# Output of a grouped-convolution chain: relay and interleaving against two passes of 32x32 transposes

## The chip, the cores and the metric

The kernel runs on one core of a Trainium2 chip. The metric is the device time of one execution in microseconds (us), the median of several.

## The reference, cut to what matters

The input x is 32 batches of 128 channels by 2048 positions, float32. Four layers are applied one after the other, each with a residual:

```
x = x + conv(x, w0, 9 taps, pad 4, groups=4) + (cond @ cw0.T + side)   # L0
x = x + einsum(agg_w1[b], x[b]) + agg_b1[b]                            # L1
x = x + einsum(agg_w2[b], x[b]) + agg_b2[b]                            # L2
x = x + conv(x, w3, 9 taps, pad 4, groups=4) + (cond @ cw3.T + side)   # L3
```

In L1 and L2 agg_w[b] is a 128x128 matrix for each batch: a softmax over 8 attention weights (from a small network on cond) mixes 8 given matrices. Each group of the convolutions maps 32 channels to 32.

## The kernel before

**Work on TensorE.** The residuals are folded into the weights, and L1 and L2 become one matrix per batch, the product (I + A2)(I + A1). A group of 32 channels fills only 32 rows of the 128x128 array. So the positions are split into PH = 4 phases, l = 4s + p with S = 512, and a matmul with 32 rows (one group) and 128 columns gives 32 output channels at all four phases at once. Each array quarter works on one group; four such matmuls run beside each other. A convolution is SHIFTS = 12 shifts by 3 products (operands are split into a high and a low part in the type fp32r: hi*hi, hi*lo, lo*hi), hence 36 rounds of four matmuls of 512 columns. Its result for group g stands in PSUM bank g; partition (p, o) or (o, p) is channel o of the group at phase p, column s. mix has 12 rounds and turns this layout back, so that z has channels on partitions and phase planes along them. The last convolution (conv3, weights of l = 0 or 1: l = 1 here) orders its 128 outputs as (o, p): partition 4o + p.

**The output before.** conv3's four banks are evacuated with their bias to out_taps by ScalarE (g = 0, 1) and VectorE (g = 2, 3; evac_out, lines 401 and 518). Four DMAs on SP's queue (relay_out, line 258) copy each group's 128x512 into 32 rows of out_planes (128 channels, 4 planes of 512). GpSimd copies out_planes to out_sb, interleaving the planes (weave_out, line 333, writes every fourth element), and SP stores out_sb, 1 MB, contiguous (line 267). The last batch has relays with semaphores of their own, and ScalarE and VectorE each weave a half (lines 306 to 319, 409, 669 to 673).

**The input before.** SP loads x[b] to x_in (line 253). GpSimd copies it to x_planes, four phase planes (plane_x, line 325, reads every fourth element). ScalarE rounds it to x_hi (high_x, line 378), VectorE subtracts to get x_lo (low_x, line 493). For x[0] VectorE makes the planes, in halves (line 602).

**Order of the work.** Each engine has its own written-out order, and semaphores tie them. In step t (t = 0 to 32):

- TensorE: conv0(t), first half of conv3(t-1), product(t+1), second half of conv3(t-1), mix(t). conv0(t) waits for x_lo(t) and for the evacuation of t-2; conv3(t-1) for z_lo(t-1); product(t+1) for the mixing matrices of t+1 and for y_lo(t); mix(t) for y_lo(t), the spread weights and the sum of the product.
- ScalarE: high_y(t), high_x(t+2), evac_out(t-1), high_z(t).
- VectorE: mix_matrices(t+1) (16 small instructions, line 526; the one for k = 7, l = 0 writes every fourth element), low_y(t), split_product(t+1) (sum, rounded part, rest), low_x(t+2), evac_out(t-1), low_z(t).
- SP: relay_out(t-2), load_x(t+4), store(t-2), spread_mix_w(t+1).
- GpSimd: plane_x(t+2), weave_out(t-2).

y is the result of conv0, z that of mix. Before the steps stand the set-up of weights and tables and the first batch: tap_blocks (line 557) makes block-diagonal tap matrices, taps_low (line 567) the low part of the turned taps. For l = 0 it writes and reads runs of 32 neighbouring elements, for l = 1 every fourth (phase_columns, line 240).

Of the kernel before, what the change touches and what calls it, by code (L numbers as in the profile page):

```python
# [31 lines left out]
G = 4  # L32
GC = C // G
TAPS, PAD = 9, 4
PH = C // GC
# [6 lines left out]
RELAY = G * DMA  # L42
# [4 lines left out]
def conditioned_residual_kernel(nc, x, cond, side, conv0_w, ctx0_w, mix1, mix2, conv3_w, ctx3_w, out):  # L47

# [4 lines left out]
    with ctx:  # L53
# [7 lines left out]
        x_planes = sb("x_planes", [C, PH, S])  # L61
# [30 lines left out]
        o0, o1 = out_sb[0], out_sb[1]  # L92
# [13 lines left out]
        op = out_planes[:, :, :].rearrange("c p s -> c (p s)")  # L106
# [4 lines left out]
        mix2_in = out_taps[:, 0:G // 2, :].rearrange("o g (k i) -> o (g k) i", i=C)  # L111
# [60 lines left out]
        x0_planed = sem("x0_planed")  # L172
        x0_high = sem("x0_high")
        x_loaded = [sem(f"x_loaded{i}") for i in range(2)]
        x_planed = sem("x_planed")
# [17 lines left out]
        out_relaid = sem("out_relaid")  # L193
        out_woven = sem("out_woven")
        last_relaid = [sem(f"last_relaid{g}") for g in range(G)]
        last_woven = [sem(f"last_woven{h}") for h in range(2)]
# [55 lines left out]
        def _(sp):  # L252
            def load_x(t, d):
                b = t.i + d
                sp.wait_ge(x_planed, b - 1)
                sp.dma_start(x_in[t.par(d)][:, :], x[b]).then_inc(x_loaded[t.par(d)], DMA)

            def relay_out(t, d):
                b = t.i + d
                sp.wait_ge(out_act, 2 * (b + 1))  # L260
                sp.wait_ge(out_dve, 2 * (b + 1))
                wait(sp, out_woven, b)
                for g in range(G):
                    sp.dma_start(out_planes[rows(g), :, :], out_taps[:, g, :])\
                      .then_inc(out_relaid, DMA)
# [16 lines left out]
            def one(t):  # L282
                if t.has(-2) and not t.at(N + 1):
                    relay_out(t, -2)
                if t.has(4):
                    load_x(t, 4)
                if t.has(-2) and not t.at(N + 1):
                    store(t, -2)
                if t.has(1):
                    spread_mix_w(t, 1)  # L290
# [9 lines left out]
            load_x(zero, 2)  # L300
            load_x(zero, 3)
            spread_mix_w(zero, 0)
            for t in ALL:
                one(t)

            b = N - 1
            for g in range(G):
                if g < 2:
                    sp.wait_ge(out_act, 2 * b + g + 1)
                else:  # L310
                    sp.wait_ge(out_dve, 2 * b + g - 1)
                if g == 0:
                    sp.wait_ge(out_woven, b)
                sp.dma_start(out_planes[rows(g), :, :], out_taps[:, g, :])\
                  .then_inc(last_relaid[g], DMA)
            for h in range(2):
                sp.wait_ge(last_woven[h], 1)
                sp.dma_start(out[b, :, h * L // 2:(h + 1) * L // 2], out_sb[b % 2][:, h * L // 2:(h + 1) * L // 2])\
                  .then_inc(out_stored[b % 2], DMA)
            sp.wait_ge(out_stored[0], DMA * (N // 2))  # L320
            sp.wait_ge(out_stored[1], DMA * (N // 2 + 1))

        @block.gpsimd
        def _(pool):
            def plane_x(t, d):
                b = t.i + d
                pool.wait_ge(x_loaded[t.par(d)], DMA * (t.pair(d) + t.par(d)))
                pool.wait_ge(x_lo_done, b)
                pool.wait_ge(x_hi_done, b)
                pool.tensor_copy(x_planes[:, :, :], x_in[t.par(d)][:, :].rearrange("c (s p) -> c p s", p=PH))\  # L330
                    .then_inc(x_planed, 1)

            def weave_out(t, d):
                b = t.i + d
                pool.wait_ge(out_relaid, RELAY * (b + 1))
                wait(pool, out_stored[t.par(d)], DMA * t.pair(d))
                pool.tensor_copy(out_sb[t.par(d)][:, :].rearrange("c (s p) -> c p s", p=PH), out_planes[:, :, :])\  # L337
                    .then_inc(out_woven, 1)

            def one(t):  # L340
                if t.has(2):
                    plane_x(t, 2)
                if t.has(-2) and not t.at(N + 1):
                    weave_out(t, -2)

# [24 lines left out]
            plane_x(Step(0, 0), 1)  # L370
            for t in ALL:
                one(t)
# [4 lines left out]
        def _(act):  # L377
            def high_x(t, d):
                b, p = t.i + d, t.par(d)
                act.wait_ge(x_planed, b + 1)  # L380
                wait(act, conv0_done, G * (b - 1))
                act.activation(x_hi[p][:, :, 1:S + 1], x_planes[:, :, :], ACT.Copy).then_inc(x_hi_done, 1)
# [18 lines left out]
            def evac_out(t, d):  # L401
                b = t.i + d
                wait(act, out_relaid, RELAY * b)
# [5 lines left out]
            def weave_last(h):  # L409
                s = slice(0, S // 2)  # L410
                act.activation(out_sb[1][:, 0:L // 2].rearrange("c (s p) -> c p s", p=PH), out_planes[:, :, s],  # L411
                               ACT.Copy).then_inc(last_woven[h], 1)
# [20 lines left out]
            def one(t):  # L433
                if t.has(0) and not t.at(0):
                    high_y(t)
                if t.has(2):
                    high_x(t, 2)
                if t.has(-1):
                    evac_out(t, -1)
                if t.has(0):  # L440
                    high_z(t)

# [17 lines left out]
            for h in range(2):  # L460
                act.wait_ge((x0_planed, x_planed)[h], 1)
                s = slice(h * S // 2, (h + 1) * S // 2)
                act.activation(x_hi[0][:, :, 1 + s.start:1 + s.stop], x_planes[:, :, s], ACT.Copy)\
                   .then_inc((x0_high, x_hi_done)[h], 1)
# [21 lines left out]
            for g in range(G):  # L486
                act.wait_ge(last_relaid[g], DMA)
            act.wait_ge(out_stored[1], DMA * (N // 2 - 1))
            weave_last(0)

        @block.vector
        def _(dve):
            def low_x(t, d):
                b, p = t.i + d, t.par(d)
                dve.wait_ge(x_hi_done, b + 1)
                dve.tensor_tensor(out=x_lo[p][:, :, 1:S + 1], in0=x_planes[:, :, :],  # L496
# [21 lines left out]
            def evac_out(t, d):  # L518
                b = t.i + d
                wait(dve, out_relaid, RELAY * b)  # L520
                for g in range(2, G):
                    dve.wait_ge(conv3_done, G * b + g + 1)
                    dve.tensor_scalar(out_taps[:, g, :], ps[:, bank(t, d) + g, :],
                                      bias_tab[:, b, G + g:G + g + 1], None, ALU.add).then_inc(out_dve, 1)
# [18 lines left out]
            def split_product(t, d):  # L543
                b = t.i + d
                dve.wait_ge(prod_done, G * (b + 1))
                wait(dve, mix_w_spread[t.par(d - 1)], RELAY * (t.pair(d - 1) + 1) if not (t.at(-d)) else 0)
# [32 lines left out]
            def one(t):  # L579
# [8 lines left out]
                if t.has(-1):  # L588
                    evac_out(t, -1)
# [12 lines left out]
            for h in range(2):  # L602
                dve.wait_ge(x0_halves[h], DMA)
                dve.tensor_copy(x_planes[:, :, h * S // 2:(h + 1) * S // 2],
                                x_in[0][:, h * L // 2:(h + 1) * L // 2].rearrange("c (s p) -> c p s", p=PH))\
                   .then_inc((x0_planed, x_planed)[h], 1)
# [3 lines left out]
            dve.wait_ge(x_planed, 1)  # L610
            for h in range(2):
                dve.wait_ge((x0_high, x_hi_done)[h], 1)
                s = slice(h * S // 2, (h + 1) * S // 2)
                half = dve.tensor_tensor(out=x_lo[0][:, :, 1 + s.start:1 + s.stop], in0=x_planes[:, :, s],
# [36 lines left out]
            dve.wait_ge(x_planed, 2)  # L651
# [17 lines left out]
            for g in range(G):  # L669
                dve.wait_ge(last_relaid[g], DMA)  # L670
            dve.wait_ge(out_stored[1], DMA * (N // 2 - 1))
            dve.tensor_copy(out_sb[1][:, L // 2:L].rearrange("c (s p) -> c p s", p=PH), out_planes[:, :, S // 2:S])\
               .then_inc(last_woven[1], 1)

        @block.tensor
        def _(pe):
# [37 lines left out]
            def mix(t):  # L714
                b, w = t.i, mix_w[t.par(0)]
                pe.wait_ge(y_lo_done, G * (b + 1))
                pe.wait_ge(mix_w_spread[t.par(0)], RELAY * (t.half + 1))
# [159 lines left out]
```

## Time and profile before

| | |
|---|---|
| median of 3 runs | 715.63 us (715.04 to 716.25) |
| profiled execution | 715.86 us |
| its span, first to last instruction | 714.1 us |
| TensorE busy | 664.8 us, 93% |
| VectorE busy | 484.8 us, 68% |
| ScalarE busy | 256.5 us, 36% |
| GpSimd busy | 253.5 us, 36% |
| mean granted TensorE clock | 0.967 |

A busy share is the part of the span in which the engine had at least one instruction running. Matmuls overlap each other, so a busy TensorE is not one at its peak. The chain of waits is followed back from the last instruction: it names at each moment the work that the end depended on. In the table of groups, the time of one instruction is from start to end; instructions on one engine overlap at their ends, so n of them take less than n times that. Line numbers (L683) are those of the kernel above.

### The profile page before, as it was taken

Reading aid. Unit: us, or ns where it says so; the run is one execution under the profiler, and the core shown is the slowest. Engines: PE = TensorE matmul, PEld = TensorE weight load, DVE = VectorE, ACT = ScalarE, POOL = GpSimd, SP = SyncE. Lnnn points to the kernel's source line nnn. Section 1 sums busy time; section 2 is a strip of 40 time slices with the busy share of each in tenths; the row PEclk is TensorE's granted clock in tenths of the full one; section 3 lists DMA queues with packets and bytes.
Section 4 is the critical chain, followed back from the end, with each engine's and each line's share of the span. In section 5 each row is a group of like instructions: output and inputs, shape, how many; then the busy total and the mean of one; then the engine's idle time right before and its main releaser. Section 6 shows DMA issues by size and latency. Waiting matters only on the chain.

```text
span 714.1 us, 24424 instructions
## 1 busy us (share of the span) xinstructions
PE 664.8 (93%) x11104; PEld 650.9 (91%) x11104; DVE 484.8 (68%) x941; ACT 256.5 (36%) x319; POOL 253.5 (36%) x94
## 2 busy tenths in 40 slices
PE   4846999999999999999999999999999999999970
PEld 4645889999999999999999999999999999999960
DVE  5378677767676667776777776787777777777221
ACT  3303433343334443434333444343443344432211
POOL 7022233343344444334334444433433444422220
PEclk9957999999999999999999999999999999999986
DMA  8131478889988888889998888888999888666666
GB/s 274 61 90 31 114 184 194 182 155 206 175 181 187 192 192 190 189 166 176 206 174 182 187 192 191 190 185 163 180 206 180 171 192 194 134 131 128 109 120 152
DMA packets 50238, 119.72 MB, mean 168 GB/s; under 512 B 5865, under 2 KB 25369, under 8 KB 42265
## 3 DMA queue, kind: packets, MB, share of 16 engines
q1 hardware_dynamic: 48592, 118.66, 77.7%
q10 hardware_dynamic: 1352, 0.57, 0.3%
q8 instruction: 22, 0.36, 0.3%
q14 instruction: 16, 0.12, 0.1%
q0 software_dynamic: 256, 0.01, 0.0%
HBM read 35.33 MB, written 33.55 MB: 96 GB/s over the span
## 4 chain that ended last, share of the span: by engine, by line
PE 91%; DVE 3%; DMA 2%; ACT 1%; issue 1%; ACTq 0%; SPq 0%; DVEq 0%
PE ps L683 77%; PE ps L724 12%; DMA out_planes<-in_L_cond_c_weight 1%; DMA out_planes<-out_taps 1%; DVE out_planes L561 1%; DVE acc L540 1%; PE ps L711 1%; PE ps L753 1%; DVE y_lo L503 0%; DVE z_lo L513 0%; DVE mat2T L540 0%; ACT out_sb L411 0%; PE ps L778 0%; DVE mat L540 0%; DVE taps_lo L569 0%
## 5 line engine op out<-in xcount | busy, mean ns | idle before, releaser
L337 POOL COPY out_sb<-out_planes 128x2048 f32<-128x2048 f32 x31 | 122.1, 3939 | 301.2 <-DMA out_planes<-out_taps 301.2
L683 PE MATMUL ps<-z_hi,taps_hi 32*128 32x512 f32 x1536 | 203.8, 402 | 3.6 <-DVE z_lo L513 3.6
L683 PE MATMUL ps<-x_hi,taps_hi 32*128 32x512 f32 x1536 | 202.2, 397 | 1.0 <-DVE prod L553 1.0
L683 PE MATMUL ps<-z_hi,taps_lo 32*128 32x512 f32 x1536 | 201.2, 394 | 0.5 <-issue 0.5
L683 PE MATMUL ps<-x_lo,taps_hi 32*128 32x512 f32 x1536 | 200.9, 394 | 0.0
L683 PE MATMUL ps<-x_hi,taps_lo 32*128 32x512 f32 x1536 | 200.7, 393 | 0.0
L683 PE MATMUL ps<-z_lo,taps_hi 32*128 32x512 f32 x1536 | 200.3, 393 | 0.0
L330 POOL COPY x_planes<-x_in 128x2048 f32<-128x2048 f32 x31 | 120.3, 3881 | 138.9 <-DVE x_lo L496 135.8
L388 ACT ACTIVATE y_hi<-ps,bias_tab 128x512 fp32r<-128x512 f32 x128 | 77.6, 690 | 213.5 <-PE ps L683 213.5
L513 DVE SCALAR_TENSOR_TENSOR z_lo<-ps,bias_tab,z_hi 128x1024 fp32r<-128x1024 f32 x64 | 79.2, 1280 | 74.9 <-ACT z_hi L398 74.9
L683 PEld LDWEIGHTS ps<-z_hi,taps_hi 32*128 32x128 f32 x1536 | 120.8, 186 | 6.1 <-DVE z_lo L513 4.0
L683 PEld LDWEIGHTS ps<-x_hi,taps_hi 32*128 32x128 f32 x1536 | 121.2, 186 | 3.0 <-DVE prod L553 1.2
L683 PEld LDWEIGHTS ps<-x_lo,taps_hi 32*128 32x128 f32 x1536 | 121.4, 187 | 1.7 <-issue 0.2
L683 PEld LDWEIGHTS ps<-x_hi,taps_lo 32*128 32x128 f32 x1536 | 121.3, 186 | 1.7
L683 PEld LDWEIGHTS ps<-z_lo,taps_hi 32*128 32x128 f32 x1536 | 121.1, 186 | 1.1
L683 PEld LDWEIGHTS ps<-z_hi,taps_lo 32*128 32x128 f32 x1536 | 120.6, 185 | 1.3
L503 DVE SCALAR_TENSOR_TENSOR y_lo<-ps,bias_tab,y_hi 128x512 fp32r<-128x512 f32 x128 | 87.3, 745 | 46.8 <-ACT y_hi L388 46.8
L724 PE MATMUL ps<-y_hi,mix_w 32*128 32x512 f32 x1024 | 98.9, 394 | 0.0
L406 ACT ACTIVATE out_taps<-ps,bias_tab 128x512 f32<-128x512 f32 x64 | 40.6, 685 | 155.7 <-PE ps L683 155.7
L398 ACT ACTIVATE z_hi<-ps,bias_tab 128x1024 fp32r<-128x1024 f32 x64 | 67.9, 1113 | 46.7 <-PE ps L724 46.7
L724 PEld LDWEIGHTS ps<-y_hi,mix_w 32*128 32x128 f32 x1024 | 72.8, 186 | 0.8
L496 DVE TENSOR_TENSOR x_lo<-x_planes,x_hi 128x2048 fp32r<-128x2048 f32 x31 | 70.8, 2285 | 0.0
(102 smaller groups left out, 566.2 us busy)
## 6 DMA issues: line engine op xcount, KB each, us to landing
out_planes<-out_taps SPq DMA_DIRECT2D x128, 256.0 KB, 7.4
x_in<-in_x SPq DMA_DIRECT2D x31, 1024.0 KB, 11.0
out<-out_sb SPq DMA_DIRECT2D x31, 1024.0 KB, 4.2
mix_w<-prod SPq DMA_DIRECT2D x128, 128.0 KB, 4.5
x_in<-in_x SPq DMA_DIRECT2D x2, 512.0 KB, 6.1
out<-out_sb SPq DMA_DIRECT2D x2, 512.0 KB, 3.1
out_taps<-in_L_cond_weight SPq DMA_DIRECT2D x1, 512.0 KB, 9.5
mix_w<-in_L_cond_weight SPq DMA_DIRECT2D x1, 512.0 KB, 13.2
```

Of the source, the lines that this page charges most:

```text
L330: pool.tensor_copy(x_planes[:, :, :], x_in[t.par(d)][:, :].rearrange("c (s p) -> c p s", p=PH))\
L337: pool.tensor_copy(out_sb[t.par(d)][:, :].rearrange("c (s p) -> c p s", p=PH), out_planes[:, :, :])\
L388: act.activation(y_hi[:, g, :], ps[:, bank(t, 0) + g, :], ACT.Identity, bias=bias_tab[:, b, g:g + 1]).then_inc(y_hi_done, 1)
L398: act.activation(z_hi[:, 2 * h:2 * h + 2, 1:S + 1], ps[:, k:k + 2, :], ACT.Identity, bias=bias_tab[:, b, 2 * G:BIAS]).then_inc(z_hi_done, 1)
L406: act.activation(out_taps[:, g, :], ps[:, bank(t, d) + g, :], ACT.Identity, bias=bias_tab[:, b, G + g:G + g + 1]).then_inc(out_act, 1)
L496: dve.tensor_tensor(out=x_lo[p][:, :, 1:S + 1], in0=x_planes[:, :, :], in1=x_hi[p][:, :, 1:S + 1].bitcast(F32), op=ALU.subtract).then_inc( ...
L503: dve.scalar_tensor_tensor(out=y_lo[:, g, :], in0=ps[:, bank(t, 0) + g, :], scalar=bias_tab[:, b, g:g + 1], in1=y_hi[:, g, :].bitcast(F32) ...
L513: dve.scalar_tensor_tensor(out=z_lo[:, 2 * h:2 * h + 2, 1:S + 1], in0=ps[:, k:k + 2, :], scalar=bias_tab[:, b, 2 * G:BIAS], in1=z_hi[:, 2 ...
L540: dve.scalar_tensor_tensor(out=o, in0=inputs[0], scalar=att_tab[:, b, K * l + k:K * l + k + 1], in1=inputs[1], op0=ALU.mult, op1=ALU.add). ...
L561: dve.tensor_copy(blocks[rows(g), :, rows(g)], conv_in[l][rows(g), :, :].rearrange("o c t -> o t c"))\
L683: tile = pe.matmul(ps[:, first_bank + g, :], w[rows(g), d, :], a[rows(g), d % PH, d // PH:d // PH + S], start=(n == 0), stop=(n == TURNS - 1))
L724: tile = pe.matmul(ps[:, bank(t, 0) + p, :], w[rows(p), g, h, :], a[rows(p), g, :], start=(n == 0), stop=(n == 3 * G - 1))
```

## The change

The output no longer goes through relay and weave. ScalarE evacuates groups 0 and 1 with bias to out_taps as before (now two groups large). VectorE then makes eight 128x512 transposes in 32x32 blocks in step t, in place of its two evacuations. The first pass takes groups 2 and 3 from PSUM, without bias, and 0 and 1 from out_taps, and writes out_turned. The second pass reads out_turned and writes out_runs, in which partition (o, i) holds for each group g the 512 contiguous positions 512i to 512i + 511 of channel o. ScalarE adds the bias of groups 2 and 3 in place (bias_runs). SP stores with one DMA a batch, in runs of 512 elements.

GpSimd has no work in the steps. x_planes is gone: high_x and low_x read x_in at every fourth element. SP's load_x waits for x_lo (b - 1 batches) in place of x_planed. The last batch is stored like the others.

```diff
-        x_planes = sb("x_planes", [C, PH, S])
-        out_taps = sb("out_taps", [C, G, S])
-        out_planes = sb("out_planes", [C, PH, S])
-        out_sb = [sb(f"out_sb{i}", [C, L]) for i in range(2)]
+        out_taps = sb("out_taps", [C, G // 2, S])
+        out_turned = sb("out_turned", [C, G, S])
+        out_runs = [sb(f"out_runs{i}", [C, G, RUN]) for i in range(2)]
...
+        def planes(buf, s):
+            return buf[:, PH * s.start:PH * s.stop].rearrange("c (s p) -> c p s", p=PH)
```

On SP's queue:

```diff
             def load_x(t, d):
                 b = t.i + d
-                sp.wait_ge(x_planed, b - 1)
+                wait(sp, x_lo_done, b - 1)
                 sp.dma_start(x_in[t.par(d)][:, :], x[b]).then_inc(x_loaded[t.par(d)], DMA)
-            def relay_out(t, d):
...
             def store(t, d):
                 b = t.i + d
-                sp.wait_ge(out_woven, b + 1)
-                sp.dma_start(out[b], out_sb[t.par(d)][:, :]).then_inc(out_stored[t.par(d)], DMA)
+                sp.wait_ge(runs_done, G * (b + 1))
+                sp.wait_ge(runs_biased, 2 * (b + 1))
+                sp.dma_start(out[b].rearrange("(g o) (i x) -> (o i) g x", g=G, i=RUNS), out_runs[t.par(d)][:, :, :])\
+                  .then_inc(out_stored[t.par(d)], DMA)
...
             def one(t):
+                if t.has(1):
+                    spread_mix_w(t, 1)
                 if t.has(4):
                     load_x(t, 4)
-                if t.has(-2) and not t.at(N + 1):
-                    store(t, -2)
-                if t.has(1):
-                    spread_mix_w(t, 1)
+                if t.has(-1):
+                    store(t, -1)
```

On ScalarE, where bias_runs(t, -1) is the last call of one(t), after high_z(t):

```diff
-                act.activation(x_hi[p][:, :, 1:S + 1], x_planes[:, :, :], ACT.Copy).then_inc(x_hi_done, 1)
+                act.activation(x_hi[p][:, :, 1:S + 1], planes(x_in[p], slice(0, S)), ACT.Copy).then_inc(x_hi_done, 1)
...
+            def bias_runs(t, d):
+                b = t.i + d
+                for g in range(2, G):
+                    act.wait_ge(runs_done, G * b + g + 1)
+                    o = out_runs[t.par(d)][:, g, :]
+                    act.activation(o, o, ACT.Identity, bias=bias_tab[:, b, G + g:G + g + 1]).then_inc(runs_biased, 1)
```

On VectorE, where turn_out(t, -1) stands in one(t) in the place of evac_out:

```diff
-                dve.tensor_tensor(out=x_lo[p][:, :, 1:S + 1], in0=x_planes[:, :, :],
+                dve.tensor_tensor(out=x_lo[p][:, :, 1:S + 1], in0=planes(x_in[p], slice(0, S)),
...
-            def evac_out(t, d):
...
+            def turned(g):
+                return out_turned[:, g, :].rearrange("c (p o b) -> c b o p", p=PH, o=SQ // PH)
+
+            def turn_out(t, d):
+                b = t.i + d
+                for g in (2, 3, 0, 1):
+                    if g >= 2:
+                        dve.wait_ge(conv3_done, G * b + g + 1)
+                        dve.transpose(turned(g), ps[:, bank(t, d) + g, :]).then_inc(out_dve, 1)
+                    else:
+                        dve.wait_ge(out_act, 2 * b + g + 1)
+                        dve.transpose(turned(g), out_taps[:, g, :]).then_inc(taps_turned, 1)
+                wait(dve, out_stored[t.par(d)], DMA * t.pair(d))
+                for n, g in enumerate((0, 1, 2, 3)):
+                    dve.wait_ge(taps_turned if g < 2 else out_dve, 2 * b + g % 2 + 1)
+                    dve.transpose(out_runs[t.par(d)][:, g, :].rearrange("c (j s p) -> c j p s", s=SQ, p=PH),
+                                  out_turned[:, g, :].rearrange("c (p r j) -> c j p r", p=PH, r=SQ))\
+                       .then_inc(runs_done, 1)
```

SQ is 32, RUNS is 4, RUN is 512. Where the head made x_planes of x[0] in halves, ScalarE and VectorE now read the halves of x_in[0] directly, and load_x of x[3] stands behind the first spread_mix_w on SP's queue.

## Rows read from the trace of the kernel before

**Rows 1.** The chain that ended last, by engine, share of the span.

```profile
PE 91%; DVE 3%; DMA 2%; ACT 1%; issue 1%; ACTq 0%; SPq 0%; DVEq 0%
```

**Rows 2.** The chain in one steady step: start us, us, what.

```profile
401.66 2.79 PE ps L724 x48
404.45 12.54 PE ps L683 x216
416.98 0.14 PE ps L711 x5
417.12 4.31 PE ps L683 x70
```

**Rows 3.** Timeline of VectorE: start us, us, what, [idle before <-releaser].

```profile
405.53 2.48 DVE L513 SCALAR_TENSOR_TENSOR z_lo<-ps,bias_tab,z_hi 128x1024 fp32r<-128x1024 f32 x2 [2.42 <-ACT z_hi L398]
407.92 0.34 DVE L540 SCALAR_TENSOR_TENSOR acc<-mix_w,att_tab,ident 128x128 f32<-128x128 f32 x1
...
411.60 0.43 DVE L540 SCALAR_TENSOR_TENSOR mat<-mix_w,att_tab,acc 128x128 f32<-128x128 f32 x1
...
413.43 2.73 DVE L503 SCALAR_TENSOR_TENSOR y_lo<-ps,bias_tab,y_hi 128x512 fp32r<-128x512 f32 x4 [1.22 <-ACT y_hi L388]
417.27 0.69 DVE L548 TENSOR_REDUCE prod_sum<-ps 128x128 f32<-128x512 f32 x1 [1.12 <-PE ps L711]
...
418.69 2.29 DVE L496 TENSOR_TENSOR x_lo<-x_planes,x_hi 128x2048 fp32r<-128x2048 f32 x1
421.47 1.41 DVE L523 TENSOR_SCALAR out_taps<-ps,bias_tab 128x512 f32<-128x512 f32 x2 [0.49 <-PE ps L683]
...
441.29 0.75 DVE L523 TENSOR_SCALAR out_taps<-ps,bias_tab 128x512 f32<-128x512 f32 x1 [0.58 <-PE ps L683]
```

**Rows 4.** Timeline of ScalarE in a steady step.

```profile
434.79 1.93 ACT L382 ACTIVATE x_hi<-x_planes 128x2048 fp32r<-128x2048 f32 x1
```

**Rows 5.** Windows of taps_lo (L569), l = 0, then l = 1: busy (instructions), clock, DMA.

```profile
11.11:12.66 1.55, 1.55 (x4) 1.00 1.01 372
55.99:58.42 2.43, 2.43 (x4) 0.95 0.00 0
```

**Rows 6.** Line 569 in the window 55 to 58.4 (l = 1), then in the whole trace.

```profile
L569 DVE TENSOR_TENSOR taps_lo<-ps,taps_hi x4: 651/669/690, 56.0 to 57.8; 128x288 fp32r<-128x288 f32 x4
...
L569 DVE TENSOR_TENSOR taps_lo<-ps,taps_hi x8: 447/554/690, 11.1 to 57.8; 128x288 fp32r<-128x288 f32 x8
```

**Rows 7.** Groups of instructions, two with strided operands: busy us, mean ns | idle before.

```profile
L604 DVE COPY x_planes<-x_in 128x1024 f32<-128x1024 f32 x2 | 2.2, 1113 | 2.0 <-DMA x_in<-in_x 2.0
...
L411 ACT ACTIVATE out_sb<-out_planes 128x1024 f32<-128x1024 f32 x1 | 2.0, 2034 | 9.8 <-DMA out_planes<-out_taps 9.8
```

**Rows 8.** The chain: mix(31), then conv3(31).

```profile
678.58 2.73 PE ps L724 x47
...
684.98 11.53 PE ps L683 x126
```

**Rows 9.** DMA issues: KB each, median us from issue to landing.

```profile
out<-out_sb SPq DMA_DIRECT2D x31, 1024.0 KB, 4.2
```

**Rows 10.** The chain in the head.

```profile
17.34 6.57 PE ps L683 x64
...
44.40 3.87 DVE out_planes L561
...
48.30 0.43 DVE out_planes L561
```

**Rows 11.** Timeline of GpSimd in the head.

```profile
44.15 3.84 POOL L330 COPY x_planes<-x_in 128x2048 f32<-128x2048 f32 x1 [25.25 <-DVE x_lo L496]
```

**Rows 12.** Timeline of VectorE in the head.

```profile
12.58 2.35 DVE L614 TENSOR_TENSOR x_lo<-x_planes,x_hi 128x1024 fp32r<-128x1024 f32 x2
```

**Rows 13.** Windows: PE, PEld, DVE, ACT, POOL busy (x), PEclk, DMA share, GB/s.

```profile
34.00:36.00 2.00, 0.00 (x0) 0.00 (x0) 1.92 (x6) 2.00 (x4) 0.00 (x0) 0.93 0.00 0
...
685.00:691.10 6.10, 6.10 (x56) 4.80 (x60) 0.00 (x0) 0.00 (x0) 0.55 (x1) 0.50 0.66 77
```

More of the change, by code:

```diff
@@ L41 @@
 DMA = 16
-RELAY = G * DMA
+SPREAD = PH * DMA
+SQ = 32
+RUNS = 4
+RUN = L // RUNS
 ATT = 2 * K
@@ L89, in conditioned_residual_kernel @@
         ones = sb("ones", [GC, C])
-        o0, o1 = out_sb[0], out_sb[1]
+        o0, o1 = (o[:, :, :].rearrange("c g x -> c (g x)") for o in out_runs)
         conv_in = [o0[:, 288 * l:288 * l + GC * TAPS].rearrange("o (c k) -> o c k", k=TAPS) for l in range(2)]
@@ L192, in conditioned_residual_kernel @@
         out_dve = sem("out_dve")
[L193 to L196, printed above, removed]
+        taps_turned = sem("taps_turned")
+        runs_done = sem("runs_done")
+        runs_biased = sem("runs_biased")
         out_stored = [sem(f"out_stored{i}") for i in range(2)]
@@ L300, in _ @@
             load_x(zero, 2)
+            spread_mix_w(zero, 0)
             load_x(zero, 3)
-            spread_mix_w(zero, 0)
             for t in ALL:
                 one(t)
[L306 to L319, printed above, removed]
             sp.wait_ge(out_stored[0], DMA * (N // 2))
-            sp.wait_ge(out_stored[1], DMA * (N // 2 + 1))
+            sp.wait_ge(out_stored[1], DMA * (N // 2))
         @block.gpsimd
         def _(pool):
[L325 to L344, printed above, removed]
             pool.memset(ident[:, :], 0.0).then_inc(ident_step, 1)
@@ L369, in _ @@
                 pool.dma_start(bias_k[l], m[7]).then_inc(bias_k_in, DMA)
-            plane_x(Step(0, 0), 1)
-            for t in ALL:
-                one(t)
         HALOS = 6
@@ L402, in evac_out @@
                 b = t.i + d
-                wait(act, out_relaid, RELAY * b)
+                wait(act, taps_turned, 2 * b)
                 for g in range(2):
@@ L441, in one @@
                     high_z(t)
+                if t.has(-1):
+                    bias_runs(t, -1)
             act.dma_start(cond_in, cond).then_inc(cond_arrived, DMA)
@@ L460, in _ @@
             for h in range(2):
-                act.wait_ge((x0_planed, x_planed)[h], 1)
+                act.wait_ge(x0_halves[h], DMA)
                 s = slice(h * S // 2, (h + 1) * S // 2)
-                act.activation(x_hi[0][:, :, 1 + s.start:1 + s.stop], x_planes[:, :, s], ACT.Copy)\
+                act.activation(x_hi[0][:, :, 1 + s.start:1 + s.stop], planes(x_in[0], s), ACT.Copy)\
                    .then_inc((x0_high, x_hi_done)[h], 1)
@@ L485, in _ @@
                 one(t)
[L486 to L489, printed above, removed]
         @block.vector
@@ L516, in low_z @@
                                              op0=ALU.add, op1=ALU.subtract).then_inc(z_lo_done, 1)
-            def evac_out(t, d):
+            def turned(g):
+                return out_turned[:, g, :].rearrange("c (p o b) -> c b o p", p=PH, o=SQ // PH)
+            def turn_out(t, d):
                 b = t.i + d
[L520 to L524, printed above, removed]
+                for g in (2, 3, 0, 1):
[11 more added lines that the diff above has]
+                       .then_inc(runs_done, 1)
             def mix_matrices(t, d):
@@ L545, in split_product @@
                 dve.wait_ge(prod_done, G * (b + 1))
-                wait(dve, mix_w_spread[t.par(d - 1)], RELAY * (t.pair(d - 1) + 1) if not (t.at(-d)) else 0)
+                wait(dve, mix_w_spread[t.par(d - 1)], SPREAD * (t.pair(d - 1) + 1) if not (t.at(-d)) else 0)
                 at = prod_at(t, d)
@@ L588, in one @@
                 if t.has(-1):
-                    evac_out(t, -1)
+                    turn_out(t, -1)
                 if t.has(0):
@@ L601, in _ @@
             dve.tensor_copy(condT, ps[:, 6, 0:N]).then_inc(condT_done, 1)
[L602 to L606, printed above, removed]
             for p in range(PH):
@@ L613, in _ @@
                 s = slice(h * S // 2, (h + 1) * S // 2)
-                half = dve.tensor_tensor(out=x_lo[0][:, :, 1 + s.start:1 + s.stop], in0=x_planes[:, :, s],
+                half = dve.tensor_tensor(out=x_lo[0][:, :, 1 + s.start:1 + s.stop], in0=planes(x_in[0], s),
                                          in1=x_hi[0][:, :, 1 + s.start:1 + s.stop].bitcast(F32), op=ALU.subtract)
@@ L650, in _ @@
             split_product(zero, 0)
-            dve.wait_ge(x_planed, 2)
             low_x(zero, 1)
@@ L668, in _ @@
                 one(t)
[L669 to L673, printed above, removed]
         @block.tensor
@@ L716, in mix @@
                 pe.wait_ge(y_lo_done, G * (b + 1))
-                pe.wait_ge(mix_w_spread[t.par(0)], RELAY * (t.half + 1))
+                pe.wait_ge(mix_w_spread[t.par(0)], SPREAD * (t.half + 1))
                 if t.has(1) and not t.at(0):
```

22 lines of the change are left out of this document (3 added, 19 removed).

## The prediction

> **What bounds the kernel now.** I read the page's busy shares and its chain first, then the chain of one step, then VectorE's timeline of the same step, then the two ends of the trace. The chain is TensorE for 91% of the span [rows 1]. In a steady step (401.66 to 421.43, 19.77 us) the chain holds only TensorE: mix 2.79, conv0 and the first half of conv3 12.54, product 0.14, second half of conv3 4.31, with no gap [rows 2]. So a gain can only come from the head and the tail, and a loss from any engine that no longer fits in 19.77 us.
>
> VectorE is that engine [rows 3]. Call E the end of a conv3 (421.43). After it come: evac_out (2 instructions, 1.41), a wait of 2.42 for z_hi, low_z (2.39 until the next start), the 16 instructions of mix_matrices (407.92 to 412.21, which is 413.43 less the 1.22 of waiting: 4.29), low_y 2.73, a wait for the product, split_product (417.27 to 418.69: 1.42), low_x 2.29, and 0.49 of waiting for E. The waits sum to some 5.3 us, but only what lies between E and low_y helps the change, since product(t+1) on TensorE waits for all of low_y(t): low_y ends at 416.16, the product starts at 416.98. Once low_y slips by more than about 0.8 us, TensorE stands still in the middle of conv3, every step.
>
> **The change, part by part.**
>
> *Added: eight 128x512 transposes a step on VectorE*, between E and low_z, in place of two evacuations. No row shows a transpose. Bound from below: of an evacuation of the same size one alone takes 0.75 us and two 1.41, so they repeat every 0.66 us [rows 3]. Bound from above: the nearest strided rows. taps_lo writes 288 elements per partition, for l=0 in rows of 32 neighbours, for l=1 at every fourth element (16 bytes), reading taps_hi in the same way. Four instructions take 1.55 us in the first case and 2.43 us in the second [rows 5]; less the last one's own 0.45 and 0.65 us (the shortest of the eight, and the shortest of the strided four [rows 6]) and over three that is 0.37 and 0.59 us each, so the strided one costs 0.59/288 = 2.05 ns an element. ScalarE shows it too: 1024 elements written at stride 4 took 2.03 us [rows 7], 2048 contiguous ones 1.93 us [rows 4]. The first pass writes with strides of 128, 16 and 1 elements, innermost 128, so no two writes in a row are neighbours; the second reads at stride 16 and writes at stride 4. Both have what the slow row has, hence 512 x 2.05 ns = 1.05, with a little between instructions 1.07 us each, 8.6 us for eight. I take this end, as the rows with the same strides are nearer than the evacuation. That taps_lo has a strided read and write at once and still costs 2.05 ns says that the two do not add up.
>
> The Trainium skill ("SBUF — State Buffer", the note on SBUF cachelines) says that SBUF works in 16-byte lines and wants two hits a line for full rate, so that fp32 at a stride of 16 bytes pays. The strided rows agree. Against it stands the rule of "VectorE: DVE Perf Modes" (Mode 1x) that the basic mode takes any stride at one result a cycle, and of "Vector Engine (DVE) Microarchitecture Reference" (3.8) that the transpose sustains one element per cycle. By those the first rival below would come true; taps_lo is the row against them.
>
> *Moved: x read in its natural order.* POOL's plane_x goes. high_x and low_x now read x_in at stride 4. For low_x the lower bound is today's 2.29, the upper 2048 x 2.05 ns = 4.2, with its start 4.3. The row for a strided read alone is x_planes at the start: 1024 in 1.11 us [rows 7], no slower than one operand in plain order would be at 0.66 us for 512 from PSUM, so it would speak for 2.29; but it is a copy of one operand from SBUF to SBUF, which may otherwise run faster, and so decides nothing. taps_lo, with two operands and strided ones, is the same kind of instruction as low_x. I take 4.3. high_x on ScalarE becomes 1.9 to 3.9; it starts 13.4 us after E (434.79 against 421.43 [rows 4]) and is hidden by VectorE, which comes later still.
>
> *The sum of a step.* From the end of low_y: product starts 0.1 later, reduce 0.29 after that, split_product 1.42, low_x 4.3 (together 6.1, against 0.1 + 0.14 + 4.31 + 0.1 = 4.65 at which conv3's end lets the turn start), turn_out 8.6, low_z 2.39, mix_matrices 4.29, low_y 2.73: 6.1 + 8.6 + 9.41 = 24.1 us. VectorE has no pause in it and sets the step: 24.1 - 19.77 = 4.33 us more. Steps t=1 to 28 have all parts: 28 x 4.33 = +121. Step 29 has no low_x: 4.65 + 8.6 + 9.41 = 22.66, +2.9. Step 30 has neither product nor matrices and stays at TensorE's pace. conv3(31) started 6.4 us after conv3(30) ended (684.98 against 678.58 [rows 8]); now turn_out(30) stands before low_z(31): 0.1 + 8.6 + 2.4 = 11.1, +4.7.
>
> *Removed at the tail: relay and weave.* From the end of conv3(31) (684.98 + 11.53 = 696.51) to the end of the span are 17.6 us: evacuation, four relays, the weave, two half stores [rows 8]. After: 0.1 + 8.6, the last bias_runs 0.7 (as an evacuation on ScalarE), issue and store 0.1 + 0.35 + 4.2 (median landing of a full store [rows 9]) = 14.1. -3.5.
>
> *Head.* tap_blocks(1) stood 3.87 us in one copy that otherwise takes 0.43, [rows 10], all of it under POOL's plane_x at 44.15 [rows 11]: with that gone, -3.4. low_x(1) before it in VectorE's queue grows by 2.0. The two low halves of x(0), 12.58 to 14.93 [rows 12], end 3.1 later (first high half +1.0, their own 2.1), at 18.0; conv0(0) started at 17.34 [rows 10]: +0.7. Net -0.7. Other moves I price at nothing: SP's load_x now waits for x_lo (VectorE, about a step and a half before the data is used, 11 us landing at most); the load of x(3) goes behind spread(0), 30 us ahead of its use; the store goes behind spread and load in SP's queue, and only two steps later does anyone wait for out_runs. bias_runs sits last in ScalarE's step behind turn_out, and behind it high_y, which then waits for conv0 or low_y anyway; if turn_out took over 11 us, high_y would come late. The relays' 1 MB a step leaves the queues, which were hidden.
>
> Sum: 121 + 2.9 + 4.7 - 3.5 - 0.7 = +124.4; 714.1 + 124.4 = 838.5 us of span, and 1.8 us around it (profiled execution 715.86, median 715.63, the same within 0.03%): **840 us**.
>
> **The rivals.**
>
> *All strides free (faster).* Eight transposes at 0.66 = 5.3, low_x 2.3. Then the turn starts at E and the loop is 4.65 + 5.3 + 9.41 = 19.36 < 19.77: TensorE keeps its pace. Gains: head -3.4, tail 17.6 - (0.1 + 5.3 + 0.7 + 4.65) = -6.8, loss before conv3(31) 0.1 + 5.3 + 2.4 - 6.4 = +1.4. 714.1 - 8.8 + 1.8 = 707. For it: the 1.11 us of the strided copy, and mix_matrices' one instruction that writes at stride 4, which at 0.43 in place of 0.34 is only a little slower [rows 3]. Against it: taps_lo. It turns into a loss when a transpose costs over 0.71 us (8T = 19.77 - 4.65 - 9.41), or low_x over 3.25.
>
> *Only one of the two directions is slow.* Only low_x: 6.1 + 5.3 + 9.41 = 20.8, +29 over 28 steps, less the ends: 739. Reads only (first pass 0.66, second 1.07, low_x 4.3): 22.4 a step, 789. Writes only (low_x 2.3): 22.66 a step and the whole gain of the head, 798.
>
> *The clock falls too.* At 24.1 us a step TensorE stands 1.2 us before conv3 and 2.8 us before the product. In the trace it ran at half its rate (1.2 GHz) for 6.1 us after the pause of 3.6 us before conv3(31), about 3 us of work lost; and where TensorE did nothing from before 34.0, the mean of 34 to 36 is already 0.93 [rows 13]. Here that would fall on conv3's second half: its end comes at 7.7 after low_y in place of 4.65, later than low_x's 6.1, so +1.6 a step, 28 x 1.6 = 45: 885 us if it happens in every step, in between if in some.
>
> *Strides of 64 and 512 bytes cost more than 16.* At 1.5 us a transpose the step is 27.5 and the time about 940. No row has such a stride in SBUF.
>
> **Chances.** Forecast (840) 0.42; clock falls as well (up to 885) 0.17; one direction only (789 to 798) 0.15; low_x only (739) 0.05; all strides free (707) 0.14; no net change, gains at the ends against a small excess of the step, 0.02; beyond 895 0.05. The range 735 to 895 leaves out the last three. The forecast's own range is 825 to 860, T from 1.03 to 1.15. Changes within 0.2% cannot be told from none here. Faster 0.14, same 0.02, slower 0.84.
>
> **What would show it.** Right: transposes of about 1.1 us, low_x about 4.3 us, VectorE over 95% busy, TensorE's waits named low_y and low_z, a period near 24 us, tap_blocks(1) in four copies of 0.43. Wrong: transposes of 0.66 us and an unchanged chain of 19.77 us a step (then about 707), or the granted clock at 0.5 for a part of each step. If the transposes take 1.07 and low_x 2.3 the mechanism holds and the time is near 798.

## Result: 799.85 us in place of 715.34

| | before | after |
|---|---|---|
| median, same chip | 715.34 us (714.86 to 716.25) | 799.85 us (797.16 to 805.11) |
| ratio, 95% | | 1.119 (1.113 to 1.125) |
| span of the profiled execution | 714.1 us | 798.6 us |
| mean granted TensorE clock | 0.967 | 0.948 |
| data moved by DMA | 119.7 MB | 86.2 MB |

The change makes the kernel 12% slower. The forecast was 840 us, its range 735 to 895. The direction and the mechanism came true; the size was 40 us too large.

The page after: first the busy shares (us, share of the span, instructions), then the chain by engine, which stands against [rows 1].

```profile
PE 695.2 (87%) x11104; PEld 625.4 (78%) x11104; DVE 711.0 (89%) x1130; ACT 364.0 (46%) x382; POOL 9.4 (1%) x32
...
DVE 75%; PE 18%; issue 4%; ACT 2%; DMA 0%; DVEq 0%; ACTq 0%
```

The chain was TensorE for 91% and is now VectorE for 75%. VectorE's busy time rose from 484.8 to 711.0 us. The page's groups (busy us, mean ns | idle before) say with what: eight transposes a step, of about 1.1 us each, and low_x at 3.8.

```profile
L491 DVE STREAM_TRANSPOSE out_runs<-out_turned 128x512 f32<-128x512 f32 x128 | 128.6, 1107 | 0.0
...
L453 DVE TENSOR_TENSOR x_lo<-x_in,x_hi 128x2048 fp32r<-128x2048 f32 x31 | 119.2, 3845 | 0.3 <-ACT x_hi L339 0.3
...
L484 DVE STREAM_TRANSPOSE out_turned<-ps 128x512 f32<-128x512 f32 x64 | 64.8, 1099 | 27.1 <-PE ps L640 27.1
```

One steady step in the chain (start, us), to be laid beside [rows 2]:

```profile
416.43 2.65 DVE y_lo L460 x4
...
419.12 0.62 PE ps L668 x8
...
419.77 0.70 DVE prod_sum L517
...
421.05 3.75 DVE x_lo L453
424.80 1.94 DVE out_turned L484 x2
426.74 0.97 DVE out_turned L487 x2
427.71 0.65 issue
428.36 4.08 DVE out_runs L491 x4
432.44 2.33 DVE z_lo L470 x2
...
438.97 2.65 DVE y_lo L460 x4
```

From one low_y to the next (416.43 to 438.97) are 22.54 us. Apart from the product of 0.62 us all of it is VectorE (in the "issue" of 0.65 the fourth transpose, which starts at 427.4 and takes 1.12, is running). Where the rows are cut, between 420.47 and 421.05, stand the cast and the rest of the product (0.24 and 0.29), and between 432.44 and 438.97 stand low_z and the 16 instructions of mix_matrices, 6.53 us. The starts of the product's sum are 22.49 to 22.59 us apart in 17 of 29 steps, 22.91 and 22.67 in two, and 23.25 to 23.31 in ten, about every third; before, 19.77 and 19.82 in turn. The mean over t = 1 to 28 is 22.79 against 19.80: 28 x 2.99 = 84 us. That is all of the difference. What the ends give and take cancels out.

TensorE's longest waits (us in total, times, longest):

```profile
PE ps L668 <- DVE y_lo L460: 52.3, 29, 2.0
...
PE ps L640 <- DVE out_turned L484: 5.6, 19, 0.7
```

It stands before the product in every step. Windows behind one such stop, with the columns of [rows 13], show what every third step has besides:

```profile
438.60:442.00 3.40, 1.57 (x35) 1.15 (x30) 3.00 (x6) 3.21 (x1) 0.00 (x0) 1.00 0.00 0
442.00:445.40 3.40, 3.40 (x44) 2.90 (x40) 3.02 (x4) 0.00 (x0) 0.00 (x0) 0.53 0.11 39
445.40:448.80 3.40, 3.40 (x64) 3.07 (x60) 2.78 (x2) 0.82 (x2) 0.00 (x0) 0.97 0.83 135
```

In the first row TensorE works for 1.57 us, stands, and is still granted 1.00. In the second it is busy throughout at a granted 0.53, nearly all of it at 1.2 GHz, and 44 matmuls fall in it where the third, nearly all at 2.4 GHz, has 64.

The two ends. The tail, from the end of conv3(31) at 785.64 to 798.6, takes 13.0 us, 17.6 before [rows 8]:

```profile
774.26 11.38 PE ps L640 x140
785.64 1.90 DVE out_turned L484 x2
...
791.10 1.94 DVE out_runs L491 x2
...
793.07 0.72 ACT out_runs L371
```

The head has lost its stall: the copies of tap_blocks(1) take 0.32 to 0.44 us, where one took 3.87 [rows 10]; low_x(1) before them grew to 3.79.

```profile
41.96 3.79 DVE x_lo L453
45.75 0.32 DVE out_turned L530
...
47.02 0.44 DVE out_turned L530
```

### The profile page after: what moved, and what is told of

The parts are those of the page before. It is cut to its first block, busy times and chain, and to the rows that moved or that the text cites. A ratio compares the mean times of both kernels' runs of the same rounds, so it can differ in the third digit from the quotient of the medians.

```text
span 798.6 us, 24419 instructions
## 1 busy us (share of the span) xinstructions
PE 695.2 (87%) x11104; PEld 625.4 (78%) x11104; DVE 711.0 (89%) x1130; ACT 364.0 (46%) x382; POOL 9.4 (1%) x32
## 4 chain that ended last, share of the span: by engine, by line
DVE 75%; PE 18%; issue 4%; ACT 2%; DMA 0%; DVEq 0%; ACTq 0%
DVE out_runs L491 15%; PE ps L640 14%; DVE y_lo L460 10%; DVE x_lo L453 9%; DVE z_lo L470 9%; DVE acc L509 8%; DVE out_turned L484 8%; DVE mat2T L509 4%; DVE out_turned L487 4%; DVE mat L509 3%; PE ps L668 2%; DVE prod_sum L517 2%; PE ps L710 1%; DVE prod L522 1%; DVE prod L520 1%
## 5 line engine op out<-in xcount | busy, mean ns | idle before, releaser
L640 PE MATMUL ps<-x_lo,taps_hi 32*128 32x512 f32 x1536 | 167.9, 394 | 0.0
L640 PE MATMUL ps<-x_hi,taps_lo 32*128 32x512 f32 x1536 | 167.5, 392 | 0.0
L491 DVE STREAM_TRANSPOSE out_runs<-out_turned 128x512 f32<-128x512 f32 x128 | 128.6, 1107 | 0.0
L339 ACT ACTIVATE x_hi<-x_in 128x2048 fp32r<-128x2048 f32 x31 | 121.4, 3917 | 0.0
L453 DVE TENSOR_TENSOR x_lo<-x_in,x_hi 128x2048 fp32r<-128x2048 f32 x31 | 119.2, 3845 | 0.3 <-ACT x_hi L339 0.3
L640 PEld LDWEIGHTS ps<-x_hi,taps_hi 32*128 32x128 f32 x1536 | 87.9, 186 | 20.1 <-issue 13.7
L640 PEld LDWEIGHTS ps<-x_hi,taps_lo 32*128 32x128 f32 x1536 | 88.2, 186 | 5.5
L640 PEld LDWEIGHTS ps<-x_lo,taps_hi 32*128 32x128 f32 x1536 | 88.1, 186 | 5.0 <-issue 0.2
L484 DVE STREAM_TRANSPOSE out_turned<-ps 128x512 f32<-128x512 f32 x64 | 64.8, 1099 | 27.1 <-PE ps L640 27.1
L355 ACT ACTIVATE z_hi<-ps,bias_tab 128x1024 fp32r<-128x1024 f32 x64 | 68.0, 1115 | 45.8 <-PE ps L681 45.8
L371 ACT ACTIVATE out_runs<-out_runs,bias_tab 128x512 f32<-128x512 f32 x64 | 46.4, 725 | 87.6 <-DVE out_runs L491 87.6
```

What stands on the lines that cost most here:

```text
L339: act.activation(x_hi[p][:, :, 1:S + 1], planes(x_in[p], slice(0, S)), ACT.Copy).then_inc(x_hi_done, 1)
L355: act.activation(z_hi[:, 2 * h:2 * h + 2, 1:S + 1], ps[:, k:k + 2, :], ACT.Identity, bias=bias_tab[:, b, 2 * G:BIAS]).then_inc(z_hi_done, 1)
L371: act.activation(o, o, ACT.Identity, bias=bias_tab[:, b, G + g:G + g + 1]).then_inc(runs_biased, 1)
L453: dve.tensor_tensor(out=x_lo[p][:, :, 1:S + 1], in0=planes(x_in[p], slice(0, S)), in1=x_hi[p][:, :, 1:S + 1].bitcast(F32), op=ALU.subtract ...
L484: dve.transpose(turned(g), ps[:, bank(t, d) + g, :]).then_inc(out_dve, 1)
L491: dve.transpose(out_runs[t.par(d)][:, g, :].rearrange("c (j s p) -> c j p s", s=SQ, p=PH), out_turned[:, g, :].rearrange("c (p r j) -> c j ...
```

## Experiments

Each ran beside the kernel before on its chip; the ratio is to that, with a 95% interval.

**1. All eight transposes plain.** Is it the number of transposes or their strides?

```diff
-dve.transpose(turned(g), ps[:, bank(t, d) + g, :])
+dve.transpose(out_turned[:, g, :], ps[:, bank(t, d) + g, :])
...
-dve.transpose(out_runs[..][:, g, :].rearrange("c (j s p) -> c j p s", s=SQ, p=PH),
-              out_turned[:, g, :].rearrange("c (p r j) -> c j p r", p=PH, r=SQ))
+dve.transpose(out_runs[..][:, g, :], out_turned[:, g, :])
```

> The changed kernel with all eight transposes reading and writing plain runs of 512 (the output's order is then not the reference's). Theory (the stride is the price, not the transpose): a transpose repeats every 0.66 us in place of 0.95, the clean step goes from 22.5 to 22.5 - 8 x 0.29 = 20.2 us, the span to about 720 (28 steps at 20.2 in place of 22.8 on average: -73, step 29, low_z(31) and the tail -2.3 each). Rival A (a transpose costs 0.95 us whatever its operands): 800 us unchanged. Rival B (half of the price is the transpose's own): near 760.

Measured: 716.34 us, ratio 1.002 (1.000 to 1.003). The steps take 20.12 us. VectorE's timeline of one turn:

```profile
404.31 1.32 DVE L484 STREAM_TRANSPOSE out_turned<-ps 128x512 f32<-128x512 f32 x2
405.54 1.27 DVE L487 STREAM_TRANSPOSE out_turned<-out_taps 128x512 f32<-128x512 f32 x2
406.73 2.46 DVE L491 STREAM_TRANSPOSE out_runs<-out_turned 128x512 f32<-128x512 f32 x4
```

Eight follow each other in 4.8 us (404.31 to 409.10), 0.60 each, in place of 7.64 and 0.95. Taking the strides away, with the same number of instructions on the same data, gives back all but 1 us of 84. So the cost is the transposes' strides. low_x, strided and 3.86 us long here too, costs these steps at most the 0.3 us by which they exceed 19.80, and the shorter ends make up for it; beside strided transposes, where VectorE has no time to spare, it costs more (experiment 3).

**2. One stride for each transpose.** Which strides, and do reading and writing add up?

```diff
+if g == 3: return out_turned[:, g, :].rearrange("c (p o b) -> c b o p", p=PH, o=SQ // PH)
+if g == 2: return out_turned[:, g, :]
+return out_turned[:, g, :].rearrange("c (x h) -> c h x", h=(4, 2)[g])
...
+if g >= 2: o = o.rearrange("c (j s p) -> c j p s", s=SQ, p=PH)
+if g % 2:  i = i.rearrange("c (p r j) -> c j p r", p=PH, r=SQ)
```

> Eight transposes with different strides in one kernel, to read each by itself (the output's order is not the reference's). First pass writes: group 2 plain, 3 strides 16 and 128, 0 every fourth element (16 bytes), 1 every second (8 bytes); reads plain. Second pass: 0 plain to plain, 1 reads strided and writes plain, 2 reads plain and writes strided, 3 both strided. Theory (each access that leaves its 16-byte line is slow, reading or writing, and the two don't add): 0.66 us for plain and for every second element, 0.95 for all others. Rival A (only writes are slow): group 1 of the second pass 0.66. Rival B (any stride is slow): the write at every second element 0.95. Rival C (they add): group 3 of the second pass above group 2.

Measured: 757.79 us in a single run. The instructions of one step by themselves (ns least/median/most):

```profile
L488 DVE STREAM_TRANSPOSE out_turned<-ps x1: 701/701/701, 405.7 to 405.7; 128x512 f32<-128x512 f32 x1
```
```profile
L491 DVE STREAM_TRANSPOSE out_turned<-out_taps x1: 683/683/683, 408.2 to 408.2; 128x512 f32<-128x512 f32 x1
```
```profile
L500 DVE STREAM_TRANSPOSE out_runs<-out_turned x1: 1076/1076/1076, 409.4 to 409.4; 128x512 f32<-128x512 f32 x1
```
```profile
L500 DVE STREAM_TRANSPOSE out_runs<-out_turned x1: 1115/1115/1115, 411.2 to 411.2; 128x512 f32<-128x512 f32 x1
```

In this order: plain on both sides (from PSUM); write at every second element; strided read with a plain write; both strided. The others are a write at every fourth element (1080), one at strides of 16 and 128 elements (1095), plain on both sides in the second pass (666) and a plain read with a write at every fourth (1070). So 8 bytes from one element to the next cost nothing (in writing), 16 bytes cost 0.4 us per 512 elements, a write with steps of 64 and 512 bytes no more than one at 16, reading at 16 bytes as much as writing, and both together no more than one. The rivals "larger strides cost more" (for writes) and "one direction only" fall here. A first pass with plain writes and a second that reads with steps of 128 and 4 elements gave no time, so whether a read with such large steps costs more stays open.

**3. The output change alone, GpSimd still making x_planes.** It takes low_x back to 2.28 us and puts a long GpSimd copy beside the transposes.

```diff
+pool.tensor_copy(x_planes[:, :, :], x_in[b % 2][:, :].rearrange("c (s p) -> c p s", p=PH))
...
-in0=planes(x_in[p], slice(0, S)),
+in0=x_planes[:, :, :],
```

> The changed output, but from x[1] on GpSimd makes x_planes as before, so high_x and low_x read plain planes. Theory (strided read of x is a term of its own): low_x 2.3 us in place of 3.85; the turn then starts at conv3's end, so only 0.8 of the 1.5 us is won: clean step 21.7 us, and GpSimd's copy stands again in front of tap_blocks(1) for 3.4 us: about 773 us. Rival (GpSimd's copies hold up VectorE's strided instructions as well): low_x 2.3 us but transposes over 0.95 us in the windows of the copies, 785 us or more.

Measured: 783.67 us, ratio 1.095 (1.093 to 1.097). The transposes beside the copy are hardly longer (2.10, 2.04 and 3.99 us for the three groups in one step, against medians of 2.03, 2.00 and 4.02 in the changed kernel), so the rival's cause is not there. Undisturbed steps take 21.8 us, as expected, against 22.5 with low_x strided; but 8 of 29 take 23.2 to 23.4, each with a fall of the clock. The mean is 22.2, and the 11 us above the expectation lie in these steps.

**4. The input change alone.** The kernel before, only x read directly; the load of x moves to the end of each step's DMA issues on SP's queue.

```diff
-            def plane_x(t, d):
...
-in0=x_planes[:, :, :],
+in0=planes(x_in[p], slice(0, S)),
```

> The kernel before with one half of the change alone: x split from its natural order (no x_planes, no plane_x), relay and weave as before. From the changed kernel's trace low_x repeats after 3.8 us and high_x takes 3.9. Theory (VectorE has room for this part): low_x ends 1 us after conv3's end, evac_out right after it ends when mix ends, low_z is not delayed: step 19.8 as before, head -3.4 (tap_blocks(1)) + 1.5 (low_x(1)): 713 us. Rival (the late evacuation holds back conv0, which needs its PSUM banks): up to 0.3 us a step, 722 us. The prediction's rival had 739 for this part, from a low_x of 4.3 us and eight transposes at 0.66 us beside it.

Measured: 776.18 us, ratio 1.085 (1.083 to 1.086). The theory's 713 and the rival's 722 were both over 50 us too low, the prediction's 739 for this part 37. The timeline of one step names what none of them had:

```profile
429.46 3.91 POOL L329 COPY out_sb<-out_planes 128x2048 f32<-128x2048 f32 x1 [18.00 <-DMA out_planes<-out_taps]
...
431.08 2.37 DVE L540 CAST prod<-prod_sum 128x128 fp32r<-128x128 f32 x1
```

The cast of the product's sum, 128 elements, takes 2.37 us and ends at 433.45, 0.08 us after GpSimd's weave copy (433.37). Over the whole trace, then over that of the changed kernel, where GpSimd copies nothing in the steps:

```profile
L540 DVE CAST prod<-prod_sum x32: 226/1274/2734, 42.1 to 717.7; 128x128 fp32r<-128x128 f32 x32
```
```profile
L520 DVE CAST prod<-prod_sum x32: 226/228/229, 41.5 to 739.7; 128x128 fp32r<-128x128 f32 x32
```

In this run 28 of the 32 casts overlap a weave copy, and each of them ends 0.07 to 0.09 us after it. The cast waits for the copy to end. The Trainium skill ("SBUF — State Buffer", Who interferes with whom) has this rule: casts and copies of VectorE may want the port pair that it shares with GpSimd, and whoever holds it has it for the whole instruction. The trace agrees, up to 2.73 us in place of 0.23. The kernel before shows it too, with casts of up to 1.42 us that end 0.07 to 0.09 us after a weave copy, but its chain does not run through them. In this kernel the late cast delays low_x (now 3.84), that delays the evacuation, and conv0 waits for its banks (the first of TensorE's waits):

```profile
PE ps L665 <- DVE out_taps L512: 34.9, 27, 2.1
```

Behind that stop the clock falls in every second step (0.57 from 440 to 444): steps of 20.4 to 20.9 and of 23.4 to 23.8, mostly in turn.

**5. The same, with the weave held back until low_x is done.** If it is the cast, this takes nearly all away. SP issues the store behind the spread and the load, which is not part of the question.

```diff
 pool.wait_ge(out_relaid, RELAY * (b + 1))
+if t.has(2):
+    pool.wait_ge(x_lo_done, t.i + 3)
```

> e5 (the kernel before with x read directly), with GpSimd's weave_out(t-2) held until low_x(t+2) is done, so that it no longer runs beside split_product's cast or low_x; on SP's queue the store goes behind spread_mix_w and load_x. Theory (e5's steps of 20.7 and 23.6 us come from VectorE's cast, which waits 1 to 2 us for GpSimd's copy, with the clock's fall behind it, and not from reading x at stride 4): the cast back at 0.23 us, all steps 19.8 to 19.9, 713 to 716 us. Rival A (the slower low_x alone makes evac_out late and conv0 waits for its banks): cast 0.23 us, but steps of 20.1 or more, over 722 us. Rival B (the lock moves to the mixing matrices): their first instruction 2 us instead of 0.34, time near 770.

Measured: 723.67 us, ratio 1.013 (1.009 to 1.016).

```profile
L542 DVE CAST prod<-prod_sum x32: 226/227/229, 40.9 to 663.6; 128x128 fp32r<-128x128 f32 x32
```

Some 53 of the 61 us were the waiting cast and the falls of the clock behind it. What is left, steps of 20.21 us on average, has another chain:

```profile
416.42 1.84 ACT y_hi L379 x3
418.25 3.78 ACT x_hi L373
...
422.06 2.49 DVE x_lo L487
...
425.81 1.43 DVE out_taps L514 x2
...
427.38 12.65 PE ps L667 x205
```

high_x, 3.9 us long, keeps low_x waiting, that the evacuation, and that conv0. Both theories held a part.

**6. The product three rounds later in conv3** (after round 21 in place of 18). The changed kernel, nothing else; VectorE's work is the same.

```diff
-            MID = TURNS // 2
+            MID = TURNS // 2 + 3
```

> The changed kernel with product(t+1) three rounds later in conv3 (MID 21 in place of 18): the same work, TensorE's pause before the product 0.7 us shorter (1.9 to 1.2), the rest of it moved before conv0. VectorE's instructions are unchanged. Theory (the steps of 23.3 us among those of 22.5 come from the clock, which falls after pauses of 1.9 us): no falls, every step 22.5, 800 - 8 = 791 to 792 us. Rival (the 0.75 us have another cause, such as a queue): 800 us as before.

Measured: 788.56 us, ratio 1.103 (1.101 to 1.105), 11 us less than the changed kernel. The steps take 22.43 to 22.54 us. TensorE's single stop has become two (in brackets, us):

```profile
399.69 0.51 PE L640 MATMUL ps<-x_hi,taps_hi 32*128 32x512 f32 x4 [0.96 <-DVE out_turned L484]
```
```profile
PE ps L668 <- DVE y_lo L460: 33.5, 29, 1.3
PE ps L640 <- DVE out_turned L484: 27.1, 29, 1.0
```

The sum of the stops is the same or larger (60.6 against 57.9 us), but no step has a fall of the clock (mean granted clock 0.972 against 0.948). So the long steps of the changed kernel come from the stop being in one piece of up to 2.0 us, and cost it some 10 us. The runs fit its length as the cause: in experiment 2 the stop is in one piece too, but of 1.0 to 1.2 us, and no clock falls there either.

**7. First pass plain, ScalarE evacuates all four groups.** Half of the strides gone, with the right output, by storing in 16 DMAs.

```diff
-def turned(g): return out_turned[:, g, :].rearrange("c (p o b) -> c b o p", p=PH, o=SQ // PH)
+dve.transpose(out_turned[:, g, :].rearrange("c (j k x) -> c k j x", j=4, k=4), out_taps[:, g, :])
...
-sp.dma_start(out[b].rearrange("(g o) (i x) -> (o i) g x", g=G, i=RUNS), out_runs[..][:, :, :])
+for n in range(16):
+    sp.dma_start(out[b].rearrange("(m o) (k x) -> m k o x", m=16, k=RUNS)[n], out_runs[..][rows(n % 4), n // 4, :])
```

> The changed kernel with a first pass that writes plain runs of 32 elements; the second reads and writes every fourth. For that the partitions of out_runs come in another order, so the store is 16 DMAs a batch, and ScalarE evacuates all four groups with their bias (no bias_runs). Same output as the reference. Theory (strides do not add within an instruction, a pass made plain is a clear gain): first pass 0.62 us each, second 0.95, clean step 22.5 - 1.3 = 21.2 us with no fall of the clock, about 753 us. Rival (16 stores on SP's queue hold up spread_mix_w and mix): step above 22, 775 us or more.

Measured: 762.14 us, ratio 1.065 (1.063 to 1.067).

```profile
403.41 2.49 DVE L472 STREAM_TRANSPOSE out_turned<-out_taps 128x512 f32<-128x512 f32 x4
405.81 4.06 DVE L477 STREAM_TRANSPOSE out_runs<-out_turned 128x512 f32<-128x512 f32 x4
```

The first pass costs 0.60 each, the second 0.97, and the step 21.27 us, as expected: the price per stride sets the time here too. The miss of 9 us is nearly all in the tail: from the end of conv3(31) at 740.57 to 760.6 are 20.0 us, since SP issues 16 stores one after the other, in 10.5 us (747.64 to 758.13).

**8. Only the ends of the change, in the kernel before.** Steps as before with relay and weave; the last batch alone goes through the eight transposes and four stores, and GpSimd's copy of x[2] waits until tap_blocks(1) is done.

```diff
+if b == 2:
+    pool.wait_ge(blocks_step, 2 * (2 + G) - 1)
...
-                if t.has(-1):
+                if t.at(N):
+                    turn_last(t)
+                elif t.has(-1):
                     evac_out(t, -1)
```

> The kernel before, its steps untouched, changed only at the ends: the last batch is put in order by the eight transposes, with a store for each group as soon as it is done, in place of relay and weave, and plane_x(2) waits until tap_blocks(1) is through. Theory (the change's gain is real but lies at the ends): head -3.4, tail from 17.6 to 7.6 + 0.4 + 3 = 11, -6.6: 705 us. Rival A (the tail is bound by the landing of the stores): 708 to 710. Rival B (the head's stall has another cause than GpSimd's copy): 3.4 more than the theory.

Measured: 706.22 us against 715.35, ratio 0.985 (0.983 to 0.987), the fastest of all. The chain of its tail:

```profile
695.71 1.25 DVE out_planes L525 x2
...
701.21 1.93 DVE out_sb L532 x2
```

The last batch goes out in four stores, one for each group, landing 2.1 us after issue (median); the tail from 695.66 to 705.8 takes 10.1 us in place of 17.6. The steps stay at 19.8. In the head the second tap_blocks has copies of 0.42 to 0.44 us. The first lost something in this execution: one copy took 4.11 us, beside GpSimd's clearing of the tap buffers, where all four took 2.09 before. So conv0(1) starts only 1.15 us earlier (63.08 in place of 64.23). Whether the 4.11 are due to the edit wasn't tried; the times of this kernel spread from 703.4 to 707.6 us.

## Why the prediction was right, and where it missed 40 us

**VectorE becomes the bound, through low_y and the product: right.** The chain, the wait named y_lo in all 29 steps, and the first experiment show it. The pause before conv3 that it also forecast (1.2 us) is absent in the steps. TensorE waits a little for PSUM banks before conv0 instead (out_turned, 5.6 us in all): conv0(t+1) needs the banks that the first pass empties, a wait that the prediction did not list. Its sign "VectorE over 95% busy" holds in the steady steps, where VectorE stands 0.70 of 22.5 us, and not over the whole span (89%).

**The price of a stride: the mechanism right, the size too high.** A transpose counted 1.07 and repeats every 0.95 us: 8.6 became 7.64, -0.96 a step. low_x counted 4.3 and takes 3.75 of the chain. From low_y's end to the turn that made 6.1, and measures 5.72 (419.08 to 424.80): -0.4. low_z, matrices and low_y 9.41, measured 9.18 (432.44 to 441.62): -0.2. Together 24.1 became 22.5. The step that was mis-sized is the rate of 2.05 ns an element, taken from an instruction of 288 elements [rows 5, 6] and multiplied by 512 and by 2048. The larger instructions show 0.95/0.512 = 1.9 and 3.75/2.048 = 1.8 ns. That a part of the short one's time does not grow with its size would explain this; it is an argument from these three sizes and was not tried by itself. The rate should have come with an allowance downward.

**"Reading and writing don't add up", read from taps_lo: right**, 1115 against 1076 and 1070 ns (experiment 2). The strided rows of VectorE against the copy's 1.11 us [rows 7]: the prediction set the copy aside as undecided and used taps_lo, which was the right row. Why that copy of 1024 strided elements is as fast as it is was not tried.

**Clock falls too: came true in every third step, at half the price.** The prediction gave 1.6 us a step; a long step costs 0.75 more (23.27 against 22.5), ten of them some 8 us. Experiment 6 shows that it hangs on the stop being in one piece.

**The ends.** The turn before conv3(31) is 10.0 us from conv3(30)'s end (764.25 to 774.26) against 11.1 forecast and 6.4 before: +3.6. Tail -4.6 against -3.5. Head: conv0(1) starts at 62.79, 64.23 before, -1.4 against -0.7. The first two are off by the mis-sized transposes, about 1 us each. In the head, conv0(0) starts 0.14 us later (17.48 against 17.34) where 0.7 was counted, and low_x(1) grew by 1.6 in place of 2.0. All three hardly weigh. The 11 us that the prediction gives as the longest landing of a load is the median of the page before; nothing hung on it (4.8 after).

Sum of the miss in us: 28 x (24.1 - 22.5) = 45 too much, +8 for the clock that the forecast did not include, and some 3 too much at the ends.

**What the prediction did not see.** It priced the freed GpSimd at a gain in the head alone. Experiments 3 to 5 show it is worth more: the input change alone costs 61 us, the output change alone 68, and both together 84, less than their sum. Without weave and plane copies nothing holds up the cast, and without the held cast the input change costs 8 us (experiment 5), so that 8 and 68 come near the 84. The long high_x was called hidden, and is hidden, but only because VectorE is slower still; with relay and weave in place it stands first in the chain behind those 8 us.

## What to carry to other kernels

Before moving work onto an engine that is second on the path, add up its chain through one loop with the stride of each operand in it: VectorE's transposes and low_x took 1.6 to 1.7 times as long here with 32-bit elements 16 bytes or more apart, and ScalarE's high_x twice as long (3.92 against 1.94 us). In the transposes it did not matter which of the two operands it was. A relayout that does not pay in the steps can pay at the end of the kernel, where nothing hides it, so try the ends of a change by themselves. Where TensorE had to stand anyway, two short stops beat one long one here (experiment 6).

## What the runs showed of the hardware

- VectorE's 32x32-block transpose of 128x512 float32 takes 0.67 to 0.70 us and repeats every 0.60 us, if both sides are contiguous or the write has 8 bytes from element to element. At 16 bytes on either side or both, or with steps of 64 and 512 bytes in the write, it takes 1.07 to 1.15 and repeats every 0.95. The Trainium skill ("SBUF — State Buffer", the note on SBUF cachelines) gives 16-byte lines and a penalty where each access opens a new one, without a price. The trace agrees, 8 bytes being free and 16 not.
- A long GpSimd copy does not slow transposes beside it (2.10 against 2.03 us for two), but stops a small cast of VectorE until it has ended (0.23 us become up to 2.73, experiment 4).
- TensorE's granted clock fell to half behind single stops of 1.74 to 2.11 us, though not behind each: in 10, 8 and 13 of 29 steps (the changed kernel, experiments 3 and 4). It fell in no step where the same loop had two stops of at most 1.3 and 1.0 us (experiment 6), or one of at most 1.2 (experiment 2).
